# Gathers of blocks 1 and 2 in fives, block 1 transposed one step later, and smaller rings, in a recommender kernel

## The chip, the cores and the metric

One core of a Trainium2 chip runs the whole kernel in one launch. The time is device time in microseconds; a profiled execution gives the span of the core's instructions and a little around it. Engines: TensorE (PE) for matmuls, its weight loads apart (PEld), VectorE (DVE), ScalarE (ACT), GpSimd (POOL), and SyncE (SP), which here only issues DMAs. ACT and GpSimd issue DMAs too. Each engine runs its instructions in the order of the program, and they wait for one another through semaphores, which a finished instruction or a landed DMA increments.

## The reference

512 rows, each with 39 indices into a table of 125000 x 16. The gathered table rows `e` (512 x 39 x 16) feed three branches, which one output layer joins:

```python
e = emb_table[feat_index]                                  # (512, 39, 16)
flat = e.reshape(512, -1)
linear_part = flat @ linear_w + linear_b
x0 = e
h1 = relu(einsum('bhd,bmd,ohm->bod', x0, x0, conv_w1) + conv_b1)    # 128 maps
nxt, hi1 = split(h1, 2, axis=1)
h2 = relu(einsum('bhd,bmd,ohm->bod', nxt, x0, conv_w2) + conv_b2)
res = concatenate([hi1, h2], axis=1).sum(axis=2)
y = relu(bn(flat @ deep_w1 + deep_b1)); y = relu(bn(y @ deep_w2 + deep_b2))
out = concatenate([linear_part, res, y], axis=1) @ out_w + out_b
```

`bn` is a batch norm over all 512 rows. All is fp32. An index that is out of the table is wrapped and clamped.

## The kernel before, in words

The batch is cut into 8 blocks of 64 rows; a block is 1024 columns (16 dimensions x 64 rows), so a tile is 128 partitions x 1024 fp32, and a matmul goes over it in two halves of 512.

**How a block comes in.** GpSimd issues 20 indirect DMAs per block (`gather`, L509), each of 128 table rows, into one half of `G`, which has two rooms. PE transposes `G` in three pieces (`transposes`, L707), ACT copies them out to `xT` and `flatT` and writes `xT` to a scratch tensor in device memory (`out_of_transposes`, L899). From there `load_fields` reads it back with six DMAs (`load_x`, L442): twice into `x2`, four times into `xa`, the fields stacked on partitions. `x2` is cut in a high and a low part (`high_x` on ACT, `low_x` on DVE or GpSimd) in `stack`, so that a matmul with a 0/1 matrix `put1` or `put2` can copy chosen fields to any partitions of `p_x` without loss (`place`, L736).

**The products.** The first einsum of a block is six tiles of kind `x`: PE places the partners in PSUM, DVE multiplies them by `xa` into the ring `placed` (`product`, L620), and PE contracts the tile with the weights into `p_n` (`contract`, L758). The squares go in apart (`squares`). ACT then takes `p_n` out in three instructions (`hi_out_of_l1`, `second_n`, `first_n`), the last of which gives the second einsum its factor. The second einsum of a block is 20 tiles. Most are of kind `d`: SP loads two fields from the scratch tensor, each spread over 64 partitions, into the ring `ring` (L486 to L499), DVE multiplies the tile in place by `p_n`, PE contracts it into `p_h2`. A few are of kind `p`: PE places the fields, ACT copies them into `placed` (`copy_fields`).

**Split tiles.** A tile is contracted either as plain fp32 or split: ACT makes a rounded high part `zh` (`high_part`), DVE or GpSimd the rest `zl` (`low_part`), and PE does three fast matmuls per half in place of one fp32 one. `DVE_LOW` and `POOL_LOW` say which places of a step are split, and on which engine.

**The order.** It is written out by hand. Stage -1 is the six x tiles of block 0. Step j (0 to 7) is the 20 tiles of block j's second einsum, mixed with the six x tiles of block j+1 at the places `X_AT[j]`; `P_AT[j]` are the places of kind `p`. Every engine walks through the same sequence of 208 tiles and does its further work at a place: (j, n) means place n of step j. `T_AT`, `T1_PE`, `T1_ACT`, `XA1_ACT`, `HIGH_X1_ACT` and `LOW_X1` place the arrival of a block: in the kernel before, block 1 is transposed at place 4 of stage -1, by PE and ACT, and its loads stand at place 5 there, behind it on ACT's queue. `D1` to `D2E` place the deep layers. PE places tiles ahead of their use, by a plan made at build time from these tables (L864 to L874).

**GpSimd's start.** It waits for the indices, issues the 40 gathers of blocks 0 and 1 one after another, waits for the transposes of block 0, and issues the 20 of block 2 (L531 to L537). Blocks 3 to 7 are gathered inside the steps, block b spread over places 2 to 24 of step b-3, its first one behind the transposes of block b-2. A DVE or PE instruction behind a semaphore waits in the queue of its engine, so everything behind it waits too; SP stops its ring loads behind the seventh until block 1 stands in the scratch tensor (L495).

Of the kernel before, what the change touches and what calls it, by code (L numbers as in the profile page):

```python
# [21 lines left out]
HALF_F = (FIELDS + 1) // 2  # L22
# [45 lines left out]
def runs(values, after):  # L68

    out = []  # L70
    for p, v in enumerate(values):
        if p and after(values[p - 1]) == v:
            out[-1][1] += 1
        else:
# [20 lines left out]

X_AT = {0: [6, 7, 9, 12, 16, 17], 1: [1, 2, 9, 11, 13, 15], 2: [0, 2, 5, 8, 10, 13], 3: [0, 2, 5, 8, 10, 13],
        4: [0, 2, 5, 8, 10, 13], 5: [0, 4, 7, 9, 12, 14], 6: [0, 2, 4, 6, 8, 10], 7: []}
P_AT = {0: [20, 24], 1: [17, 20, 25], 2: [17, 19, 25], 3: [17, 19, 25], 4: [17, 19, 25], 5: [], 6: [], 7: []}  # L100

DVE_LOW = {-1: [], 0: [3, 8, 13, 24], 1: [3, 12, 25], 2: [12, 20, 25], 3: [12, 20, 25], 4: [12, 20, 25],
           5: [1, 15, 23, 25], 6: [1, 12, 22, 25], 7: [0, 3, 6, 10, 27]}
POOL_LOW = {-1: [], 0: [14, 23], 1: [0, 4, 8, 10, 16, 20], 2: [1, 3, 7, 16, 19, 24], 3: [1, 3, 7, 16, 19, 24],
# [3 lines left out]

SQ_AFTER = 3


T_AT = {0: 10, 1: 6, 2: 6, 3: 6, 4: 6, 5: 6}
T_AHEAD, XA_BEHIND, HIGH_X_BEHIND, LOW_X_BEHIND = 4, 7, 11, 12
LOW_X_ON_DVE = [3]

T1_PE, T1_ACT, XA1_ACT, HIGH_X1_ACT, LOW_X1 = (-1, 4), (-1, 4), (-1, 5), (0, 2), (0, 2)
SQ_ACT_AHEAD, SQ_DVE_AHEAD = 5, -1
HI_BEHIND, DUP_BEHIND, N_BEHIND, HI_SUM_BEHIND, H2_PLACE, H2_SUM_PLACE = 3, 7, 8, 5, 1, 6
LOW_BEHIND, COPY_AHEAD, PLACE_AHEAD = 1, 3, 6
RING, PLACED_RING, HIGH_RING, LOW_RING = 9, 4, 6, 5  # L120

FIRST_LOADS = 7
D1 = [(5, 13), (5, 17), (6, 13), (6, 17)]
D1B = [(5, 20), (5, 23), (6, 20), (6, 23)]
D1S = [(5, 22), (5, 25), (6, 22), (6, 23)]
D1E = [(6, 23), (6, 25), (6, 26), (6, 26)]
D2 = [(7, -1), (7, 3), (7, 4), (7, 6)]
D2B = [(7, 6), (7, 7), (7, 9), (7, 11)]
D2S = [(7, 7), (7, 9), (7, 10), (7, 12)]
D2E = [(7, 13), (7, 12), (7, 13), (7, 14)]  # L130

# [4 lines left out]
def order_of(j):  # L136

    if j < 0:
        return [('x', 0, t) for t in range(X_TILES)]
    xs, ps = X_AT[j], dict(zip(P_AT[j], range(L2_TILES - len(P_AT[j]), L2_TILES)))  # L140
    loaded = iter([t for t in [TAIL, *range(L2_PAIRS)] if t not in ps.values()])
# [21 lines left out]

DVE_SPLITS = [s for s, (j, n) in enumerate(WHERE) if n in DVE_LOW[j]]
POOL_SPLITS = [s for s, (j, n) in enumerate(WHERE) if n in POOL_LOW[j]]
SPLITS = sorted(DVE_SPLITS + POOL_SPLITS)
# [19 lines left out]
def build(nc, idx, emb, lin_w, lin_b, w1a, w1b, b1, w2, b2, dw1, db1, g1, be1, dw2, db2, g2, be2,  # L186
# [12 lines left out]
    with ctx:  # L199
# [85 lines left out]
        s_gather = [sem("s_gather0"), sem("s_gather1")]  # L285
# [6 lines left out]
        s_tp = sem("s_tp")  # L292
# [42 lines left out]
        def own_wait(eng, semaphore, value):  # L335

            eng.wait_ge(semaphore, value)
            eng.sem_inc(s_past, 1)
# [48 lines left out]

        T_PE = {b: (b - 2, T_AT[b - 2] - T_AHEAD) for b in range(2, BLOCKS)}
        T_ACT = {b: (b - 2, T_AT[b - 2]) for b in range(2, BLOCKS)}
# [118 lines left out]
        def _(pool):  # L508
            def gather(b, f):  # L509

                nc.gpsimd.indirect_dma_start(  # L511
                    G[:, b % 2, DIM * f:DIM * (f + 1)], None, emb[:, :],
                    bass.IndirectOffsetOnAxis(idx_all[:, b, f:f + 1], 0)).then_inc(s_gather[b % 2], 16)
# [15 lines left out]
            nc.gpsimd.affine_select(out=ident[:, :], in_=ident[:, :], compare_op=ALU.not_equal, fill=1.0,  # L529
                                    base=0, pattern=[[-1, 128]], channel_multiplier=1).then_inc(s_ident, 1)  # L530
            pool.wait_ge(s_clamp, 3)  # L531
            for b in range(2):
                for f in range(HALF_F):
                    gather(b, f)
            own_wait(pool, s_tp, 1)
            for f in range(HALF_F):
                gather(2, f)  # L537

            works = each(LOW_X_POOL, low_x)
            for s, (j, n) in enumerate(WHERE):  # L540
# [556 lines left out]
```

## Time and profile before

| what | us |
|---|---|
| three runs | 499.76, 503.05, 506.67 (median 503.05) |
| profiled execution, in all | 504.29 |
| its span | 502.5 |
| PE busy | 414.9 (83%) |
| DVE busy | 370.7 (74%) |
| GpSimd (POOL) busy | 337.6 (67%) |
| ACT busy | 195.1 (39%) |
| mean granted TensorE clock | 0.948 |
| read from device memory | 88.37 MB |

The page cuts the span in 40 slices of 12.6 us; a digit is a tenth of a slice that the engine was busy, or a tenth of full clock that PE was granted. "Idle before" stands in brackets behind an instruction, with what ended it; `issue` means that the engine waited for nothing that the profile shows, and `remote` that a semaphore came whose sender the profile can't name. In a row `x4` after PE counts matmul records; an fp32 tile has four, a split one six.

### The profile page before, as it was taken

How to read it: one execution, taken by the hardware profiler on the slowest of the kernel's cores; microseconds unless marked ns; L12 is line 12 of the kernel's file. 1: busy time of each engine (PE TensorE's matmuls, PEld its weight loads, DVE VectorE, ACT ScalarE, POOL GpSimd, SP SyncE). 2: the span in 40 equal slices, each digit the busy share in tenths (PEclk: the TensorE clock that was granted, in tenths of full speed). 3: DMA queues.
4: the chain of work that ended last, by engine and by line, in shares of the span. 5: the costliest groups of instructions: out<-in, count | busy, mean ns of one | idle time of the engine just before them, and what ended most of it. 6: DMA issues, size and time to landing. Idle time of an engine off the chain costs nothing.

```text
span 502.5 us, 4581 instructions
## 1 busy us (share of the span) xinstructions
PE 414.9 (83%) x1248; PEld 232.1 (46%) x1248; DVE 370.7 (74%) x354; ACT 195.1 (39%) x242; POOL 337.6 (67%) x236
## 2 busy tenths in 40 slices
PE   0004622499999999999999999999999999999985
PEld 0002210145545655555555555564556665655713
DVE  5303010389779799889989989998878899899931
ACT  1202000333255164245415450734336357576431
POOL 5777774055776885878688868861555189867690
PEclk9999955599999999999999999999999999999978
DMA  3936831498999988899989999998786989999400
GB/s 72 170 42 149 183 49 5 102 224 192 223 218 201 235 209 199 199 199 241 218 185 218 219 227 174 230 242 220 190 209 170 237 209 229 241 253 255 125 1 0
DMA packets 42398, 89.99 MB, mean 179 GB/s; under 512 B 16012, under 2 KB 21451, under 8 KB 42372
## 3 DMA queue, kind: packets, MB, share of 16 engines
q1 hardware_dynamic: 28637, 80.28, 64.5%
q0 software_dynamic: 5120, 1.32, 7.3%
q10 hardware_dynamic: 8615, 8.09, 7.1%
q8 instruction: 10, 0.16, 0.2%
q14 instruction: 16, 0.13, 0.1%
HBM read 88.37 MB, written 1.28 MB: 178 GB/s over the span
## 4 chain that ended last, share of the span: by engine, by line
PE 60%; issue 10%; another core or an unknown queue 9%; DVE 8%; ACT 5%; SPq 3%; DMA 3%; POOL 2%; ACTq 0%; DVEq 0%; POOLq 0%
PE p_h L775 34%; PE p_n L775 13%; PE p_x L754 4%; DVE ring L643 4%; PE p_x L839 3%; PE p_n L839 3%; POOL zl L525 2%; SPq L453 1%; DVE placed L643 1%; DMA x<-xs_scratch 1%; ACT zh L958 1%; PE p_n L854 1%; DMA w2s<-in_w 1%; DVE zl L612 1%
## 5 line engine op out<-in xcount | busy, mean ns | idle before, releaser
L511 POOL DMA_INDIRECT G<-in_emb,idx_all x160 | 167.8, 1049 | 55.9 <-issue 43.0
L525 POOL TENSOR_TENSOR zl<-ring,zh 128x1024 fp32r<-128x1024 f32 x60 | 145.5, 2440 | 82.5 <-ACT zh L958 78.2
L643 DVE TENSOR_TENSOR ring<-p_n,ring 128x1024 f32<-128x1024 f32 x146 | 172.5, 1215 | 10.4 <-ACT p_n L984 9.4
L958 ACT ACTIVATE zh<-ring 128x1024 fp32r<-128x1024 f32 x83 | 87.0, 1056 | 122.1 <-DVE ring L643 84.2
L775 PE MATMUL p_h<-ring,w2s 128*128 128x512 f32 x252 | 118.0, 602 | 6.9 <-DVE ring L643 6.9
L775 PE MATMUL p_n<-placed,w1s 125*128 125x512 f32 (+2 forms) x192 | 95.0, 620 | 9.6 <-DVE placed L643 9.6
L643 DVE TENSOR_TENSOR placed<-xa,p_x 125x1024 f32<-125x1024 f32 (+2 forms) x45 | 54.6, 1214 | 37.5 <-remote 15.1
L775 PEld LDWEIGHTS p_h<-ring,w2s 128*128 128x128 f32 x252 | 48.4, 193 | 57.8 <-issue 45.3
L775 PE MATMUL p_h<-zh,w2l 128*128 128x512 f32 x184 | 68.6, 454 | 2.0 <-ACT h2s L992 0.7
L754 PE MATMUL p_x<-stack,put 103*125 103x512 f32 (+3 forms) x118 | 52.5, 527 | 10.3 <-issue 10.3
L775 PE MATMUL p_h<-zh,w2h 128*128 128x512 f32 x184 | 57.9, 396 | 0.0
L775 PEld LDWEIGHTS p_n<-placed,w1s 125*128 125x128 f32 (+2 forms) x192 | 37.8, 198 | 42.7 <-issue 28.1
L775 PE MATMUL p_h<-zl,w2h 128*128 128x512 f32 x168 | 54.0, 403 | 4.0 <-POOL zl L525 2.7
L775 PEld LDWEIGHTS p_h<-zh,w2l 128*128 128x128 f32 x184 | 33.9, 189 | 22.5 <-issue 11.9
L612 DVE TENSOR_TENSOR zl<-ring,zh 128x1024 fp32r<-128x1024 f32 x20 | 38.8, 1938 | 2.7 <-ACT zh L958 2.7
L775 PEld LDWEIGHTS p_h<-zh,w2h 128*128 128x128 f32 x184 | 34.6, 188 | 8.4
L775 PEld LDWEIGHTS p_h<-zl,w2h 128*128 128x128 f32 x168 | 30.9, 188 | 14.0 <-POOL zl L525 5.7
L754 PEld LDWEIGHTS p_x<-stack,put 103*125 103x125 f32 (+3 forms) x118 | 22.0, 191 | 31.6 <-issue 26.9
L714 PE MATMUL p_x<-ident,G 128*128 128x128 f32 (+1 forms) x21 | 3.8, 295 | 34.1 <-DMA G<-in_emb,idx_all 34.1
L973 ACT ACTIVATE placed<-p_x 128x1024 f32<-128x1024 f32 x14 | 14.4, 1027 | 35.1 <-PE p_x L754 27.5
L647 DVE TENSOR_REDUCE h_sum<-h2s 128x64 f32<-128x1024 f32 x8 | 15.5, 1937 | 15.2 <-ACT h2s L992 15.2
L518 POOL TENSOR_TENSOR stack<-x,stack 39x1024 fp32r<-39x1024 f32 x6 | 14.3, 2380 | 13.1 <-ACT stack L949 12.1
(95 smaller groups left out, 299.7 us busy)
## 6 DMA issues: line engine op xcount, KB each, us to landing
ring<-xs_scratch SPq DMA_DIRECT2D x292, 256.0 KB
xa<-xs_scratch ACTq DMA_DIRECT2D x21, 156.0 KB
G<-in_emb,idx_all POOLq DMA_INDIRECT x160
x<-xs_scratch ACTq DMA_DIRECT2D x14, 156.0 KB
xs_scratch<-xT ACTq DMA_DIRECT2D x16, 64.0 KB
dw_sb<-in_dw SPq DMA_DIRECT2D x4, 200.0 KB
xa<-xs_scratch SPq DMA_DIRECT2D x3, 156.0 KB
xa<-in_dw ACTq DMA_DIRECT2D x2, 156.2 KB
```

Of the source, the lines that this page charges most:

```text
L453: eng.dma_start(dst[p:p + n, t, :], src[row:row + n, tile, :]).then_inc(s_w, 16)
L511: nc.gpsimd.indirect_dma_start(G[:, b % 2, DIM * f:DIM * (f + 1)], None, emb[:, :], bass.IndirectOffsetOnAxis(idx_all[:, b, f:f + 1], 0)). ...
L518: nc.gpsimd.tensor_tensor(stack[0:FIELDS, b % 3, :], x2[0:FIELDS, :], stack[0:FIELDS, b % 3, :].bitcast(F32), ALU.subtract).then_inc(s_low ...
L525: nc.gpsimd.tensor_tensor(low_of(s), z_of(s), high_of(s).bitcast(F32), ALU.subtract).then_inc(s_low_pool, 1)
L612: nc.vector.tensor_tensor(low_of(s), z_of(s), high_of(s).bitcast(F32), ALU.subtract).then_inc(s_low_dve, 1)
L643: nc.vector.tensor_tensor(z_of(s), by, x, ALU.mult).then_inc(s_z, 1)
L647: return nc.vector.tensor_reduce(dst[:, ROWS * b:ROWS * (b + 1)], src.rearrange("p (d b) -> p b d", d=DIM), AX.X, ALU.add)
L754: last = nc.tensor.matmul(acc[0:rows_of(s), BANK * c:BANK * (c + 1)], put, stack[:, b % 3, BANK * c:BANK * (c + 1)], start=True, stop=True)
L775: return nc.tensor.matmul(acc[:, BANK * c:BANK * (c + 1)], w, x[:, BANK * c:BANK * (c + 1)], start=start, stop=stop)
L839: last = nc.tensor.matmul(p_d[0:end - HID_K * t, :], w[:, HID_K * t:end], x, start=c == 0, stop=c == len(parts) - 1)
L958: nc.scalar.activation(high_of(s), z_of(s), ACT.Copy).then_inc(s_zh, 1)
L973: nc.scalar.activation(z_of(s), p_x[:, :], ACT.Copy).then_inc(s_copy, 1)
```

## The change

GpSimd's gathers of blocks 1 and 2 go in groups of five (`AT_ONCE`): before each group but a block's first it waits until all gathers of the block so far have landed. Block 0 is gathered as before. Block 1 is transposed at place 0 of step 0 by PE and ACT, no longer at place 4 of stage -1; its loads, high part and low part come at places 2, 4 and 4 of step 0. The x tiles of block 1, the transposes of block 2 and the places of later work move with it. Blocks 1, 3 and 7 have their low part of `x2` on DVE, not block 3 alone. Step 0 has no split tile on GpSimd any more, step 1 three in place of six; entries beyond a step's last place do nothing, so that 88 tiles are split in place of 92. `ring` has 8 rooms in place of 9, `placed` 2 in place of 4, and ACT copies a `p` tile 2 places ahead in place of 3.

```diff
-X_AT = {0: [6, 7, 9, 12, 16, 17], 1: [1, 2, 9, 11, 13, 15], 2: [0, 2, 5, 8, 10, 13], 3: [0, 2, 5, 8, 10, 13],
+X_AT = {0: [5, 10, 12, 14, 16, 17], 1: [5, 6, 9, 11, 13, 15], 2: [0, 2, 5, 8, 10, 13], 3: [0, 2, 5, 8, 10, 13],
         4: [0, 2, 5, 8, 10, 13], 5: [0, 4, 7, 9, 12, 14], 6: [0, 2, 4, 6, 8, 10], 7: []}
-P_AT = {0: [20, 24], 1: [17, 20, 25], 2: [17, 19, 25], 3: [17, 19, 25], 4: [17, 19, 25], 5: [], 6: [], 7: []}
-
-DVE_LOW = {-1: [], 0: [3, 8, 13, 24], 1: [3, 12, 25], 2: [12, 20, 25], 3: [12, 20, 25], 4: [12, 20, 25],
-           5: [1, 15, 23, 25], 6: [1, 12, 22, 25], 7: [0, 3, 6, 10, 27]}
-POOL_LOW = {-1: [], 0: [14, 23], 1: [0, 4, 8, 10, 16, 20], 2: [1, 3, 7, 16, 19, 24], 3: [1, 3, 7, 16, 19, 24],
-            4: [1, 3, 7, 16, 19, 24], 5: [3, 8, 11, 13, 16, 19, 21, 22, 24],
+P_AT = {0: [21, 24], 1: [16, 20, 25], 2: [17, 20, 25], 3: [17, 20, 25], 4: [17, 20, 25], 5: [], 6: [], 7: []}
+
+DVE_LOW = {-1: [], 0: [3, 6, 8, 13, 24], 1: [2, 12, 25], 2: [12, 20, 25], 3: [12, 20, 25], 4: [12, 20, 25],
+           5: [1, 15, 23, 25], 6: [1, 12, 22, 25], 7: [0, 3, 6, 10, 17]}
+POOL_LOW = {-1: [], 0: [], 1: [0, 10, 24], 2: [1, 4, 7, 14, 18, 24], 3: [1, 4, 7, 14, 18, 24],
+            4: [1, 4, 7, 14, 18, 24], 5: [3, 8, 11, 13, 16, 19, 21, 22, 24],
             6: [5, 7, 9, 11, 13, 14, 15, 16, 18, 19, 20, 21, 23, 24],
-            7: [1, 2, 4, 5, 7, 8, 9, 11, 12, 13, 15, 16, 17, 18, 19, 24]}
+            7: [1, 2, 4, 5, 7, 8, 9, 11, 12, 13, 14, 16, 18, 19, 24, 29]}
...
-T_AT = {0: 10, 1: 6, 2: 6, 3: 6, 4: 6, 5: 6}
+T_AT = {0: 15, 1: 3, 2: 6, 3: 6, 4: 6, 5: 6}
 T_AHEAD, XA_BEHIND, HIGH_X_BEHIND, LOW_X_BEHIND = 4, 7, 11, 12
-LOW_X_ON_DVE = [3]
-
-T1_PE, T1_ACT, XA1_ACT, HIGH_X1_ACT, LOW_X1 = (-1, 4), (-1, 4), (-1, 5), (0, 2), (0, 2)
+LOW_X_ON_DVE = [1, 3, 7]
+
+AT_ONCE = 5
+
+T1_PE, T1_ACT, XA1_ACT, HIGH_X1_ACT, LOW_X1 = (0, 0), (0, 0), (0, 2), (0, 4), (0, 4)
...
-LOW_BEHIND, COPY_AHEAD, PLACE_AHEAD = 1, 3, 6
-RING, PLACED_RING, HIGH_RING, LOW_RING = 9, 4, 6, 5
+LOW_BEHIND, COPY_AHEAD, PLACE_AHEAD = 1, 2, 6
+RING, PLACED_RING, HIGH_RING, LOW_RING = 8, 2, 6, 5
...
-D1E = [(6, 23), (6, 25), (6, 26), (6, 26)]
-D2 = [(7, -1), (7, 3), (7, 4), (7, 6)]
-D2B = [(7, 6), (7, 7), (7, 9), (7, 11)]
+D1E = [(6, 23), (6, 26), (6, 26), (6, 26)]
+D2 = [(7, -1), (7, 3), (7, 4), (7, 4)]
+D2B = [(7, 6), (7, 7), (7, 8), (7, 11)]
...
             pool.wait_ge(s_clamp, 3)
-            for b in range(2):
+            for b in range(3):
+                if b == 2:
+                    own_wait(pool, s_tp, 1)
                 for f in range(HALF_F):
+                    if b and f and f % AT_ONCE == 0:
+
+                        own_wait(pool, s_gather[b % 2], 16 * (HALF_F * (b // 2) + f))
                     gather(b, f)
-            own_wait(pool, s_tp, 1)
-            for f in range(HALF_F):
-                gather(2, f)
```

## Rows read from the trace of the kernel before

**Rows 1.** The page's slices: busy tenths of PE, and its granted clock.
```profile
PE   0004622499999999999999999999999999999985
PEclk9999955599999999999999999999999999999978
```
**Rows 2.** Stretches: length, each engine's busy time (instructions), granted clock, DMA share, GB/s.
```profile
108.40:149.14 40.74, 40.74 (x121) 22.16 (x120) 33.61 (x28) 14.33 (x20) 27.50 (x23) 1.00 0.95 213
...
97.00:103.00 6.00, 5.12 (x7) 2.25 (x8) 5.97 (x5) 0.08 (x1) 0.00 (x0) 0.56 0.94 210
```
**Rows 3.** The chain of waits in order of time: start, length, what.
```profile
46.89 43.39 another core or an unknown queue
```
**Rows 4.** Timeline of the hole: start, length, engine, line, operation, tiles, idle before.
```profile
53.20 1.03 PE L754 MATMUL p_x<-stack,put 103*125 103x512 f32 x2
55.38 1.03 PE L754 MATMUL p_h<-stack,put 103*117 103x512 f32 x2
69.85 1.22 DVE L643 TENSOR_TENSOR placed<-xa,p_x 125x1024 f32<-125x1024 f32 x1 [15.13 <-remote]
76.74 0.85 PE L714 MATMUL p_n<-ident,G 128*128 128x128 f32 x3
...
82.08 0.94 POOL L511 DMA_INDIRECT G<-in_emb,idx_all  x1 [0.30 <-issue]
85.95 1.22 DVE L643 TENSOR_TENSOR placed<-xa,p_h 117x1024 f32<-117x1024 f32 x1 [13.75 <-remote]
90.31 0.59 ACT L903 ACTIVATE xT<-p_n 128x128 f32<-128x128 f32 x3 [43.42 <-remote]
```
**Rows 5.** Timeline: last gather of block 0, first of block 1, and early work.
```profile
31.02 0.94 POOL L511 DMA_INDIRECT G<-in_emb,idx_all  x1 [0.30 <-issue]
32.27 0.95 POOL L511 DMA_INDIRECT G<-in_emb,idx_all  x1 [0.31 <-issue]
34.07 0.87 PE L714 MATMUL p_x<-ident,G 128*128 128x128 f32 x3 [34.07 <-DMA G<-in_emb,idx_all]
48.51 1.22 DVE L643 TENSOR_TENSOR placed<-xa,p_x 125x1024 f32<-125x1024 f32 x1 [0.18 <-issue]
```
**Rows 6.** DMA from 0 to 57.05, then to 136.10: packets, MB, share; issues.
```profile
q0 software_dynamic: 1167, 0.30, 19.4%
...
q0 software_dynamic: 2348, 0.61, 14.0%
...
G<-in_emb,idx_all POOLq DMA_INDIRECT x78
```
**Rows 7.** The chain, PE's pieces: a placement, an unsplit tile, a split tile.
```profile
110.58 0.46 PE p_x L754 x2
111.04 1.72 PE p_h L775 x4
...
116.99 1.41 PE p_h L775 x6
```
**Rows 8.** Timeline: block 1 from the transposes' copy to its stack and squares.
```profile
93.17 1.11 ACT L965 ACTIVATE hi<-p_n,b_sb 64x1024 f32<-64x1024 f32 x1 [1.61 <-issue]
94.56 17.19 SPq L498 DMA_DIRECT2D ring<-xs_scratch  x14
95.60 0.75 ACTq L445 DMA_DIRECT2D x<-xs_scratch  x2
96.60 4.62 DVE L643 TENSOR_TENSOR ring<-p_n,ring 128x1024 f32<-128x1024 f32 x4 [9.43 <-ACT p_n L984]
102.92 1.06 ACT L949 ACTIVATE stack<-x 103x1024 fp32r<-103x1024 f32 x1 [6.42 <-DMA x<-xs_scratch]
106.75 1.06 ACT L929 ACTIVATE hi<-xa 39x1024 f32<-39x1024 f32 x1 [1.83 <-DMA xa<-xs_scratch]
```
**Rows 9.** The page's groups: busy, mean ns of one, idle before.
```profile
L617 DVE TENSOR_TENSOR stack<-x,stack 39x1024 fp32r<-39x1024 f32 x2 | 3.5, 1750 | 17.3 <-issue 17.3
```
**Rows 10.** The waits, who waited for whom: us in total, times, longest.
```profile
DVE ring L643 <- DMA ring<-xs_scratch: 0.3, 1, 0.3
```

## The prediction

> **What bounds the kernel now.** I read the page's slices first, then stretches of the span, the chain of waits, and only then the timeline from 26 to 112 us. The slices show PE at 9 tenths from the ninth on, and nearly empty in the sixth and seventh, with the granted clock at 5 tenths there [rows 1]. From 108.40 to 149.14 us PE was busy 40.74 of 40.74 us [rows 2]: what lies behind the first 100 us is PE's, and there only less PE work takes time out. Ahead of it stands one hole: a single piece of the chain, 43.39 us from 46.89 us, with no releaser that the profile knows [rows 3].
>
> The timeline tells what kind of hole it is [rows 4]. PE placed x tile 4 from 53.20, 1.03 us long; DVE's product of it started at 69.85, 15.13 us idle before it. Tile 5 was placed from 55.38; its product started at 85.95. The transposes of block 1 ran at 76.74; ACT, which waited for them alone, started at 90.31. Each time the work was done 13 to 30 us before the waiter moved: signals from PE are held. What runs through all of it is GpSimd, which issues a gather each 1.25 us without a pause up to 82.08; all is free 8.2 us after that last one. Later, gathers run 7 to 10 in a row beside a PE without idle time, so gathers alone don't hold it; a long unbroken row may. That is inferred from order in time; no row shows the mechanism.
>
> **The change, part by part.** Sums are against the profiled execution: span 502.5 us, 504.29 us in all, 1.2 us over the median of 503.05.
>
> *Waits for each five.* Block 0 is gathered as before. Block 1 starts at 32.27. Five take 4 x 1.25 us to the fifth's issue, then its landing L. L from below: 3.05 us (issue 31.02, PE's start on it 34.07) [rows 5]. From above: by 136.10 us 78 gathers were issued and 2348 packets, of 32 each, seen, so 4.6 in flight, 5.8 us; by 57.05, under ring loads, 39 were issued (20 of block 0, then one each 1.25 us from 32.27) with 1167 packets, 2.5 in flight, 3.2 us and so some 3.5 with the last packets' way [rows 6]. I take 3.05 for block 1's first two fives, 3.5 for the others (nearest rows): fifths landed at 40.3, 48.5, 57.1, 65.7. Block 2 follows without a wait at its head: 72, 81, 90 and, with 5 us under full DMA, about 100, where it ended at 85 before. Those 15 us are GpSimd's; behind them in its queue stands only block 3, which it then issues in one run of 20, about 97 to 121, since step 0 has no low parts on GpSimd any more.
> Of waits behind a DMA the Trainium skill says, in DMA: Bandwidth & Descriptors, section Rules for kernel authors, to issue early and wait late, and gives some 2.0 us of fixed cost (section Anatomy of one DMA). By that alone six waits would be an estimated 12 us lost and nothing won; the rows agree that there is a fixed cost, at 3.05, not that it is on the path.
>
> *Stage -1 without the hole.* Placed x4 at 54.2, product 55 to 56.2, the squares' low part to 57.4, product 5 to 58.6. PE: tile 3 to 58.1, squares 0.5, tiles 4 and 5 at 1.72 us each [rows 7]: 62.0. A ring of two for placed tiles makes product s wait for PE's tile s-2, done one tile time before: nothing here, at most 1 us. ACT's three evictions of p_n take 3.4 us (93.17 to DVE's next start at 96.60) [rows 8]: 65.4, against 96.5 before. They no longer queue behind the wait for the transposes, which is moved past them. First product of step 0 to 66.6, PE to 68.4, transposes of block 1 to 69.1; its gathers landed at 65.7 (at 76 with L at 5.8 in all four).
>
> *Block 1 on its way.* ACT's four scratch writes landed 4.25 us after the transposes were seen (90.31 to SP's next load at 94.56). The six x loads, now behind tile 2 of step 0 on ACT's queue, gave x2 7.3 us after their issue (95.60 to 102.92), and xa 11.15 us (to 106.75) [rows 8]. SP's ring loads from the eighth on start at the same landing, as before. So 69.1 + 4.25 + 7.3 = 80.7; ACT's high part 1.06; low part, now DVE's, 1.75 [rows 9]: 83.5, xa at 84.5. PE gets to the first placement behind tile 2 of step 0, at about 72, and stands there until 84. This is the new stall, 12 us, and what is late in it are the x loads. It also halves the clock: after the old hole PE had 0.56 of it from 97 to 103, which costs 2.5 us, and I charge the same [rows 2].
>
> *Rest of step 0.* Old: behind 108.40 stood tiles 4 to 25, without a gap, to 149.14. New, from 84: tiles 3 to 25, one unsplit tile more (1.72), clock 2.5, transposes of block 3 0.3: 129.3. Gain 19.9. PE comes to the transposes of block 2 (place 11) at 84 + 3 x 1.41 + 6 x 1.72 + 4 x 0.46 + 2.5 = 103 [rows 7], gathers there at 100; to those of block 3 (place 25) at 129 against 121 + 5: both just hidden. If not, PE waits in order.
>
> *Edits with small terms.* Four split tiles less (one in step 0, inside the count above, three in step 1): an unsplit tile costs PE 1.72, a split one 1.41, so 0.9 us lost. Blocks 1 and 7's low part on DVE, and one split of step 7 moved to it, lie under PE. Ring 9 to 8: a load is issued one tile, about 2 us, later; DVE lost 0.3 us in all to ring loads [rows 10]; from 0 to 3 us lost, I take 1. Copying 2 ahead in place of 3, and the shifted places of steps 1 to 4: 0 to 1. The end (deep layer up to 2 places earlier, GpSimd one tile less): from 2 won to 1 lost, taken as 0.
>
> Sum: 19.9 - 0.9 - 1 = 18.0. Span 484.5, 486.3 in all, 485 on the median's scale. Its own bounds: x loads faster by 4 and the end by 2 give 478; the small losses at their ends and L somewhat longer give 490.
>
> **Rivals.**
> *1, slower: the signals stay held as long as block 2's gathers go on.* For it: two of PE's signals came through only behind the last gather, 3.9 and 8.2 us after its issue, while a pause after a five lasts just L. Against it: x tile 2 was signalled at once (product at 48.51, idle 0.18) in the middle of the same run [rows 5]. Price with the holding just as long as before: tile 5 of stage -1 ends at 91 and ACT's evictions come 2 us earlier; but the transposes stand behind the first tile of step 0, which at half clock ends near 99, so 10 later; the placement of block 1 comes at 114.5 and not 108.4, one tile more (1.7), clock 2.5, 0.9: 11 us lost, 515. With the waits the last issue of block 2 is 14 us later: 529. It decides at tile 5's product, about 59: if that comes after 90, it is this one.
> *2, no change: the run of 20 of block 3.* It has no wait, and PE is then in full stream. If holding starts inside it (from 103, say), PE loses up to 121 + 8.2 - 103 = 26 us, half of it in the middle: 498 (486 to 511). Against: runs of 7 to 10 with PE at 40.74 of 40.74 [rows 2]; for: nothing between 10 and the row of 60 was seen beside a busy PE. The Trainium skill, in VectorE: DVE Perf Modes, section The TRN2 errata, warns that increments at a high rate from one engine can deadlock another and wants them spaced; by that rule spacing blocks 1 and 2 is right and this unspaced run is the risk. The held signals agree in kind, though nothing hung.
> *3, the waits become the bound.* L near 5 in every five: block 1 late by 4 to 7, block 2 past PE at place 11 by 5: 496, between 490 and 500. For it: DMA is at 0.95 of its time from 108 on [rows 2].
>
> **Numbers.** My forecast 0.58, rival 3 0.11, rival 2 0.15, rival 1 0.16. Two per cent, 10 us, is about what a measurement here tells from no change: under 493 is faster, over 513 slower. Faster: 0.57 + 0.07 + 0.04 = 0.68; slower: 0.16 + 0.02 = 0.18; 0.14 between. The range from 477 to 508 takes the forecast, rival 3 and most of rival 2, and leaves rival 1 out.
>
> **What would show it.** In the new trace: gathers of blocks 1 and 2 in fives, with idle of about L released by the gather's DMA; products 4 and 5 before 60 us with no unknown releaser over 2 us; ACT's transposes of block 1 near 69; PE idle from about 72 to 84 for the stack of block 1, behind the loads of x; half clock for some 5 us behind it; eviction of step 0 near 130. The forecast is wrong if products 4 or 5 are still 10 us behind their placement, if PE shows idle released by nobody between 97 and 130, or if PE waits for G at places 11 or 25.

## The result, and the profile after

The changed kernel took 521.24 us (median of four runs, 518.87 to 523.54) against 504.83 for the kernel before beside it: a ratio of 1.033 with a 95% interval of 1.029 to 1.038. It is slower by 16.4 us, where 18 less were forecast, and the range of 477 to 508 missed it. The profiled execution took 521.02 us in all, with a span of 519.2. Lines of the changed kernel are 2 to 4 higher than before's: the gather is L513, the transposes L718, a placement L758, VectorE's product L647, ScalarE's copy of a placed tile L977.

The hole that the prediction was about is gone. Its slices against [rows 1]:

```profile
PE   0005754839389999999999999998999999979975
PEclk9999977987879999999999999999999999979988
```

PE is no longer near empty in the sixth and seventh slice (5 and 4 tenths for 2 and 2), but the ninth and eleventh stand at 3, where before's are at 9. The stretch that was full before [rows 2] shows it (length, busy time of PE, PEld, DVE, ACT, POOL, granted clock, DMA share, GB/s):

```profile
108.40:149.14 40.74, 21.44 (x48) 10.82 (x49) 13.19 (x12) 4.41 (x10) 23.85 (x25) 0.75 0.41 70
```

PE is busy 21.4 of 40.7 us at 0.75 of its clock. The chain of waits says behind what, in place of the one piece of [rows 3] (start, length, what):

```profile
46.74 8.24 DMA G<-in_emb,idx_all
...
61.62 3.04 DMA G<-in_emb,idx_all
...
70.45 3.00 DMA G<-in_emb,idx_all
...
81.38 11.15 DMA xa<-xs_scratch
...
120.46 22.96 another core or an unknown queue
```

The timeline gives the rest (start, length, engine, line, operation, tiles, idle time before it and who ended it). It answers [rows 4, 5, 8]:

```profile
55.65 1.22 DVE L647 TENSOR_TENSOR placed<-xa,p_x 125x1024 f32<-125x1024 f32 x1 [0.96 <-PE p_n L779]
55.78 0.94 POOL L513 DMA_INDIRECT G<-in_emb,idx_all  x1 [8.09 <-DMA G<-in_emb,idx_all]
57.92 1.21 DVE L647 TENSOR_TENSOR placed<-xa,p_h 117x1024 f32<-117x1024 f32 x1
...
73.58 0.53 PE L718 MATMUL p_n<-ident,G 128*128 128x128 f32 x3 [3.03 <-DMA G<-in_emb,idx_all]
74.14 0.59 ACT L907 ACTIVATE xT<-p_n 128x128 f32<-128x128 f32 x3 [8.44 <-PE p_n L718]
...
86.64 1.22 PE L758 MATMUL p_x<-stack,put 103*125 103x512 f32 x2 [7.40 <-issue]
92.62 1.22 DVE L647 TENSOR_TENSOR placed<-xa,p_x 125x1024 f32<-125x1024 f32 x1 [6.04 <-DMA xa<-xs_scratch]
95.53 0.94 POOL L513 DMA_INDIRECT G<-in_emb,idx_all  x1 [8.12 <-DMA G<-in_emb,idx_all]
107.74 0.94 POOL L513 DMA_INDIRECT G<-in_emb,idx_all  x1 [4.87 <-DMA G<-in_emb,idx_all]
116.78 0.87 PE L718 MATMUL p_x<-ident,G 128*128 128x128 f32 x3 [8.44 <-DMA G<-in_emb,idx_all]
...
128.51 0.73 PE L758 MATMUL p_x<-stack,put 103*128 103x512 f32 x2 [0.70 <-issue]
138.62 0.94 POOL L513 DMA_INDIRECT G<-in_emb,idx_all  x1 [0.30 <-issue]
143.55 1.02 ACT L977 ACTIVATE placed<-p_x 128x1024 f32<-128x1024 f32 x1 [24.60 <-remote]
144.62 1.22 PE L758 MATMUL p_x<-stack,put 103*128 103x512 f32 x2 [10.22 <-ACT placed L977]
```

Four things are to be seen. The products of x tiles 4 and 5 run at 55.65 and 57.92 and not at 69.85 and 85.95: the old hold is gone. The wait for a five to land is 3 us in some places and 8 us in others. PE waits for block 2's gathers until 116.78. And from 107.74 GpSimd issues 25 gathers in a row (the last five of block 2, the twenty of block 3), and there a tile that PE had placed by 129.24 is copied only at 143.55, 4.9 us behind the last issue: the hold of the kernel before, in a new place. The copy waits for two counts of PE, that of the placed tile and that of the product which last used its room; in the second trace of the changed kernel the tile, placed by 129.98, was counted at 140.03, and the copy started at 143.66 with the last of three late counts of products (143.54 to 143.66). With a `placed` ring of 2 that product is a newer one than with 4; what this adds was not tried apart. The waits together (who waited for whom; total us, times, longest):

```profile
POOL G L513 <- DMA G<-in_emb,idx_all: 29.9, 6, 8.1
ACT placed L977 <- remote: 24.6, 1, 24.6
PE p_n L843 <- DMA G<-in_dw: 3.1, 1, 3.1
```

The last tile of step 0 ends at 158.88 (before: 149.14), that of step 1 at 208.66 (197.06), that of step 6 at 454.57 (441.65), the last of all at 511.98 (495.23). So 9.7 us are lost by the end of step 0, 3.2 in steps 1 to 6, 3.8 in step 7.

Of the kernels below, three had executions over 1.5% above their fastest, at much the same granted clock (before with six waits on PE's signals: 508.4 and 511.75 us beside 494.0 to 496.21; before with more such waits: 503.72 beside 495.44 to 501.67; the changed kernel waiting for the five before the last: 526.72 beside 518.76 to 526.28); the medians below take them in, the ratios leave them out, and the traces of the first two are of such executions.

### The profile page after: what moved, and what is told of

It reads as the page before. It is cut to its first block, busy times and chain, and to the rows that moved or that the text cites. A ratio compares the mean times of both kernels' runs of the same rounds, so it can differ in the third digit from the quotient of the medians.

```text
span 519.2 us, 4551 instructions
## 1 busy us (share of the span) xinstructions
PE 423.6 (82%) x1240; PEld 233.6 (45%) x1240; DVE 376.6 (73%) x358; ACT 190.8 (37%) x238; POOL 320.0 (62%) x228
## 4 chain that ended last, share of the span: by engine, by line
PE 51%; issue 12%; DVE 11%; POOL 9%; DMA 9%; another core or an unknown queue 4%; ACT 3%; ACTq 1%; DVEq 0%; POOLq 0%
PE p_h L779 29%; PE p_n L779 9%; POOL G L513 7%; DVE ring L647 6%; PE p_x L758 4%; DMA G<-in_emb,idx_all 3%; PE p_x L843 3%; PE p_n L843 3%; DMA G<-in_dw 3%; DMA xa<-xs_scratch 2%; DVE placed L647 2%; POOL zl L527 2%; ACT zh L962 1%; DVE zh L611 1%
## 5 line engine op out<-in xcount | busy, mean ns | idle before, releaser
L513 POOL DMA_INDIRECT G<-in_emb,idx_all x160 | 168.5, 1053 | 76.4 <-issue 41.0
L527 POOL TENSOR_TENSOR zl<-ring,zh 128x1024 fp32r<-128x1024 f32 x58 | 141.3, 2450 | 110.0 <-ACT zh L962 103.4
L647 DVE TENSOR_TENSOR ring<-p_n,ring 128x1024 f32<-128x1024 f32 x146 | 172.9, 1215 | 11.1 <-ACT p_n L988 7.7
L962 ACT ACTIVATE zh<-ring 128x1024 fp32r<-128x1024 f32 x80 | 83.9, 1055 | 154.5 <-DVE ring L647 120.2
L779 PE MATMUL p_h<-ring,w2s 128*128 128x512 f32 x264 | 128.3, 620 | 4.8 <-DVE ring L647 4.8
L779 PE MATMUL p_n<-placed,w1s 125*128 125x512 f32 (+2 forms) x192 | 92.8, 608 | 0.0
L647 DVE TENSOR_TENSOR placed<-xa,p_x 125x1024 f32<-125x1024 f32 (+2 forms) x45 | 54.6, 1213 | 41.7 <-PE p_x L758 16.6
L779 PEld LDWEIGHTS p_h<-ring,w2s 128*128 128x128 f32 x264 | 52.3, 200 | 57.2 <-issue 48.2
L758 PE MATMUL p_x<-stack,put 103*125 103x512 f32 (+3 forms) x118 | 51.5, 519 | 30.1 <-ACT placed L977 10.4
L779 PE MATMUL p_h<-zh,w2h 128*128 128x512 f32 x176 | 55.9, 399 | 0.0
L779 PE MATMUL p_h<-zl,w2h 128*128 128x512 f32 x160 | 52.2, 408 | 2.9 <-POOL zl L527 2.8
L758 PEld LDWEIGHTS p_x<-stack,put 103*125 103x125 f32 (+3 forms) x118 | 22.0, 195 | 52.6 <-issue 34.3
L616 DVE TENSOR_TENSOR zl<-ring,zh 128x1024 fp32r<-128x1024 f32 x19 | 30.3, 1595 | 15.8 <-issue 9.6
L718 PE MATMUL p_x<-ident,G 128*128 128x128 f32 (+1 forms) x21 | 4.2, 317 | 42.5 <-DMA G<-in_emb,idx_all 42.5
L977 ACT ACTIVATE placed<-p_x 128x1024 f32<-128x1024 f32 x14 | 14.4, 1025 | 40.0 <-remote 24.6
L647 DVE TENSOR_TENSOR placed<-p_n,placed 128x1024 f32<-128x1024 f32 x14 | 17.0, 1217 | 16.1 <-ACT placed L977 13.3
L718 PEld LDWEIGHTS p_x<-ident,G 128*128 128x128 f32 (+1 forms) x21 | 2.7, 148 | 46.0 <-issue 45.7
```

The source lines that it names most:

```text
L513: nc.gpsimd.indirect_dma_start(G[:, b % 2, DIM * f:DIM * (f + 1)], None, emb[:, :], bass.IndirectOffsetOnAxis(idx_all[:, b, f:f + 1], 0)). ...
L527: nc.gpsimd.tensor_tensor(low_of(s), z_of(s), high_of(s).bitcast(F32), ALU.subtract).then_inc(s_low_pool, 1)
L616: nc.vector.tensor_tensor(low_of(s), z_of(s), high_of(s).bitcast(F32), ALU.subtract).then_inc(s_low_dve, 1)
L647: nc.vector.tensor_tensor(z_of(s), by, x, ALU.mult).then_inc(s_z, 1)
L718: last = nc.tensor.transpose(room_of_t(b)[0:r, 128 * q:128 * (q + 1)], G[:, b % 2, 128 * q:128 * q + r], ident[:, :])
L758: last = nc.tensor.matmul(acc[0:rows_of(s), BANK * c:BANK * (c + 1)], put, stack[:, b % 3, BANK * c:BANK * (c + 1)], start=True, stop=True)
```

## The experiments

Every kernel was compared with the kernel before on the same chip. That turned out to matter most: before itself took 504 to 506 us in four of the six comparisons and 485 to 486 in two. I call the first kind held and the second free; one chip was met in both kinds, so it is not the chip alone. Pairs of one program in both kinds say where the difference sits. The changed kernel without waits ends step 0 at 133.00 us in its free trace and at 162.49 in its held one, and from there to the end of step 6 it takes 295.3 and 295.9 us. So it is not a clock or a memory that is slower throughout. Medians in us, ratios with 95% intervals:

| kernel | free: this / before | held: this / before |
|---|---|---|
| changed kernel | not run | 521.24 / 504.83, 1.033 [1.029, 1.038]; 521.19 / 504.4, 1.032 [1.028, 1.036] |
| changed, no waits between fives | 493.8 / 485.37, 1.017 [1.010, 1.023] | 525.78 / 504.4, 1.043 [1.038, 1.048] |
| changed, wait for the five before the last | not run | 523.93 / 504.4, 1.030 [1.025, 1.036] |
| changed, block 3 behind VectorE's products | 508.16 / 485.37, 1.043 [1.036, 1.050] | 519.71 / 505.84, 1.026 [1.019, 1.033] |
| changed, block 3 in fives too | 516.99 / 485.37, 1.062 [1.055, 1.070] | 519.1 / 505.03, 1.028 [1.023, 1.033] |
| changed, no waits, rings and tail of before | not run | 520.49 / 505.84, 1.025 [1.016, 1.033] |
| changed, waits on PE's signals instead | not run | 503.49 / 505.03, 0.999 [0.996, 1.002] |
| before, with the waits between fives | 509.85 / 485.37, 1.047 [1.039, 1.055] | 511.66 / 505.84, 1.010 [1.007, 1.013] |
| before, six waits on PE's signals | 487.2 / 486.01, 1.003 [1.000, 1.006] | 496.21 / 505.84, 0.978 [0.969, 0.986] |
| before, more such waits | 490.12 / 486.01, 1.010 [1.006, 1.013] (tighter ones) | 498.77 / 505.03, 0.987 [0.980, 0.995] |

**Block 3 in fives too.** Theory A was then: a long row of gathers holds PE's signals, always.

```diff
                     if f == 0:
                         own_wait(pool, s_tp, b - 1)
+                    if b == 3 and f and f % AT_ONCE == 0:
+                        own_wait(pool, s_gather[b % 2], 16 * (HALF_F * (b // 2) + f))
                     gather(b, f)
```

> The changed kernel with block 3's gathers in fives too, each five waiting for the last to land. Theory A (PE's signals arrive late while GpSimd issues a long unbroken row of gathers, and a pause lets them through): no signal of PE is late by over 3 us between 120 and 145, the waits of 24.6 and 12.75 us on the placed tile go, and the time is 505 to 512 against 521. Rival B (the late signals come from the new order of the work or from the smaller rings): the hold stays and the time is 518 to 524. Rival C (the landing waits themselves are what costs): three more waits of 3 to 8 us each delay block 3 as well, and the time is 520 to 530.

516.99 us, 6.2% over a before of 485.37. No signal was held, as A says, but the time is not A's; and since nothing was held in this comparison even in long rows (next kernel), the absence says nothing for A.

**No waits at all.** `AT_ONCE = 100`: order, places and rings of the change alone.

> The changed kernel without its waits between fives: the new order and the rings of 8 and 2 alone, and 60 gathers of blocks 1, 2 and 3 in one row. Theory A: one hold from about 54 to the end of the row (31 + 60 x 1.25 = 106, plus 5 to 8), so 108 to 114, some 20 us longer than before's, and the time is 524 to 545. Rival B (order and rings cost, the waits do not matter): 518 to 524, with PE going on by 90. Rival C (the landing waits are the cost): faster than the changed kernel, 500 to 515.

493.8 us, rival C's side, and theory A falls with it. GpSimd issued 63 gathers in one row from 28.03 to 109.19, the longest of all, and nothing was held (timeline):

```profile
54.51 1.22 DVE L647 TENSOR_TENSOR placed<-xa,p_h 124x1024 f32<-124x1024 f32 x1 [1.74 <-PE p_n L779]
56.70 1.22 DVE L647 TENSOR_TENSOR placed<-xa,p_x 125x1024 f32<-125x1024 f32 x1 [0.96 <-PE p_n L779]
58.97 1.21 DVE L647 TENSOR_TENSOR placed<-xa,p_h 117x1024 f32<-117x1024 f32 x1
72.69 0.94 POOL L513 DMA_INDIRECT G<-in_emb,idx_all  x1 [0.30 <-PE p_n L718]
109.19 1.96 POOL L513 DMA_INDIRECT G<-in_emb,idx_all  x1 [0.30 <-issue]
```

**The kernel before with the waits of the change**, its order and rings kept.

```diff
-            for b in range(2):
+            for b in range(3):
+                if b == 2:
+                    own_wait(pool, s_tp, 1)
                 for f in range(HALF_F):
+                    if b and f and f % 5 == 0:
+                        own_wait(pool, s_gather[b % 2], 16 * (HALF_F * (b // 2) + f))
                     gather(b, f)
```

> The kernel before with the waits between fives in blocks 1 and 2 alone; order, places and rings stay as before. Theory A: the hold to 86 to 90 goes, but PE meets the transposes of block 1 ahead of the products and waits for their landing until about 72 to 75, 14 us earlier than before; some of it is given back at block 2's transposes: 490 to 502. Rival B (order and rings cost some 15 us and the waits none): 485 to 490. Rival C (the landing waits cost as much as the hold): 503 to 512.

509.85 against 485.37: the waits alone cost 24 us where nothing is held. That is in rival C's band of 503 to 512, but not by its argument, since there was no hold whose gain they could have eaten up.

**Block 3 behind VectorE's products.**

```diff
+                    if b == 3 and f % 2 == 0:
+                        own_wait(pool, s_z, s - 1)
                     gather(b, f)
```

> The changed kernel with block 3's gathers in twos, each two waiting for VectorE's product two places before theirs, and not for a landing. Theory A: the row of 25 is broken without any landing wait, no signal of PE is late by over 3 us after 120, and the time is 503 to 511. Rival B: hold stays, 518 to 524. Rival C (landing waits): 505 to 515 only if the fives of blocks 1 and 2 are what costs, otherwise unchanged.

508.16, inside theory A's 503 to 511, but by luck: the pacing bound nothing. In the trace the 25 gathers from 107.15 to 139.00 still stand in one row, no idle time over 0.31 us in it, and no signal was held all the same. So this kernel stands for the changed kernel in a free comparison, where that one was not run: it too would be 4.3% slower than before. Against the kernel without waits (493.8) in the same comparison, the landing waits of blocks 1 and 2 cost 14.4 us where nothing is held, and block 3's (516.99) another 8.8.

**The same kernels where before takes 504.** Because before had been 19 us faster than ever, the next four were forecast by a new theory, A2: whether signals are held in a long row is a property of the comparison, not of the code.

> The kernel before, unchanged, profiled beside the others on one chip, since before took 485 us beside the last four kernels and 504 beside the changed kernel. Theory A2 (the hold of PE's signals is not a property of the row of gathers alone: it appears on some chips and not on others): where before takes 483 to 489 its trace has no stretch in which ScalarE and VectorE wait for a remote signal, and stage -1 ends by 80 and not 91; where it takes 500 to 507 the hold is there. Rival (the chips differ in clock or DMA alone): the hold is in both, and the 19 us are spread over the span.

504.01, and the hold is there: `ACT xT L903 <- remote` 43.2 us, 43.4 in the first trace.

> The changed kernel, unchanged, beside before on the same chip. Theory A2: on a chip without the hold it has no 24.6 us wait for a remote signal, and takes 506 to 511, as the kernel with block 3's gathers paced by VectorE (508), which differs in that alone: ratio 1.04 to 1.05. On a chip with the hold: 519 to 523 against 500 to 507. Rival (the hold is the row's own): 521 on any chip.

521.19: the loss of the first comparison, repeated.

> The new order and rings without the waits between fives, once more, beside before and the changed kernel. Theory A2: without a hold 493 to 496, and the waits alone are then 13 to 15 us of the loss; with a hold (chip of the first comparison) 60 gathers in a row make it 520 to 540. Rival (landing waits cost nothing, order and rings do): within 1% of the changed kernel.

525.78, 32 us more than the same program in the free comparison. Its timeline, to be laid beside the one above:

```profile
62.08 1.22 DVE L647 TENSOR_TENSOR placed<-xa,p_h 124x1024 f32<-124x1024 f32 x1 [10.15 <-issue]
78.18 1.22 DVE L647 TENSOR_TENSOR placed<-xa,p_x 125x1024 f32<-125x1024 f32 x1 [14.88 <-remote]
87.98 1.22 DVE L647 TENSOR_TENSOR placed<-xa,p_h 117x1024 f32<-117x1024 f32 x1 [7.46 <-remote]
...
103.09 0.95 POOL L513 DMA_INDIRECT G<-in_emb,idx_all  x1 [20.49 <-PE p_n L718]
```

Three products stand 7.6, 21.5 and 29.0 us later than there, behind the same gathers 1.25 us apart. The waits between fives gain 4.6 us here (525.78 to 521.19); they take the first hold out and pay it back.

> The changed kernel, but each five waits for the five before the last one (never over 10 gathers on their way, no pause for a landing), in blocks 1, 2 and 3. Where an issue takes 1.25 us and a landing 3 to 9, the wait binds little: 494 to 500 on a chip without the hold if the landing waits are what costs; 506 to 511 if any limit on gathers on their way costs as much; on a chip with the hold 515 to 540.

The gathers of each five signal one of two semaphores in turn, and GpSimd waits for the five before the last. It waited for landings 3.3 us in all, and the time stayed at 523.93: a bound on gathers on their way that lets GpSimd go on issuing frees nothing. Its first 43 gathers (28.1 to 81.9) stayed one row.

**The fives of before, again, now beside a held before.**

> The kernel before with the landing waits in fives for blocks 1 and 2 alone, once more for the other kind of chip (510 against 485 on the first). Theory A2: where before takes 500 to 507, it takes the same 506 to 513, since it has no long row left and so no hold: the 43 us wait for a remote signal is gone and the landings cost what it gave. Rival (order or place, not the row, makes the hold): 520 or more, with waits for a remote signal in stage -1.

511.66, and 509.85 in the free comparison: with no long row left it hardly matters which kind it is, which is what A2 said. The rival is out. Some counts of PE are late in this held trace too, behind its rows of 8 and 10, but by little (a tile placed by 124.56 was counted at 125.86), and no wait for a remote signal on a tile or a copy stands in it. What it pays is in its timeline:

```profile
56.21 0.94 POOL L511 DMA_INDIRECT G<-in_emb,idx_all  x1 [8.47 <-DMA G<-in_emb,idx_all]
73.13 0.87 PE L715 MATMUL p_n<-ident,G 128*128 128x128 f32 x3 [11.91 <-DMA G<-in_emb,idx_all]
108.71 2.35 POOL L518 TENSOR_TENSOR stack<-x,stack 39x1024 fp32r<-39x1024 f32 x1
111.11 1.22 PE L755 MATMUL p_x<-stack,put 103*125 103x512 f32 x2 [20.17 <-POOL stack L518]
```

PE waits 11.9 us at the transposes for block 1's landing, and 20.2 us for block 1's low part of x, which stands on GpSimd's queue behind all the waits. The change had moved that part to VectorE.

**Block 3 behind VectorE, again.**

> The changed kernel with block 3's gathers in twos behind VectorE's products, once more for the other kind of chip (508 on the first). Theory A2: where the changed kernel takes 519 to 523, the row of 25 is what holds the signals from 128 to 143, and pacing it gives 505 to 511. Rival (the pacing does not pause GpSimd long enough): 517 to 523 with the wait of 20 us or more for a remote signal still there.

519.71: a miss for A2. The waits were met when GpSimd reached them, so the row was never broken (106.52 to 138.44, no idle time over 0.31 us in it), and the hold stayed:

```profile
143.42 1.02 ACT L979 ACTIVATE placed<-p_x 128x1024 f32<-128x1024 f32 x1 [24.71 <-remote]
```

The same program with the same row, free and then held, is the clearest sight of what a hold takes (stretches as above):

```profile
124.00:144.40 20.40, 20.39 (x53) 9.66 (x52) 17.47 (x15) 8.37 (x8) 14.03 (x14) 1.00 0.74 151
124.00:144.40 20.40, 9.44 (x25) 4.13 (x23) 5.06 (x5) 0.98 (x1) 11.72 (x13) 0.86 0.26 31
```

Step 0 ends at 144.39 in the free trace and at 158.69 in the held one; step 1 gives 2.3 us of that back.

**Rings of 9 and 4 and the tail's loads of before, no waits.**

```diff
-RING, PLACED_RING, HIGH_RING, LOW_RING = 8, 2, 6, 5
+RING, PLACED_RING, HIGH_RING, LOW_RING = 9, 4, 6, 5
...
-D1E = [(6, 23), (6, 26), (6, 26), (6, 26)]
-D2 = [(7, -1), (7, 3), (7, 4), (7, 4)]
-D2B = [(7, 6), (7, 7), (7, 8), (7, 11)]
+D1E = [(6, 23), (6, 25), (6, 26), (6, 26)]
+D2 = [(7, -1), (7, 3), (7, 4), (7, 6)]
+D2B = [(7, 6), (7, 7), (7, 9), (7, 11)]
```

> The changed kernel without its waits, and with the rings of 9 and 4 and the four loads of the tail placed as in before: what is left of the change is the order of the tiles and splits. If rings and tail cost most of the 8.4 us between this order without waits (494) and before (485) on a chip without the hold: 485 to 488 there, and 517 to 522 against 526 on a chip with it. If the order costs it: 492 to 495, or 524 to 528.

520.49, in the band of "rings and tail", and 5.3 us under the kernel without waits (525.78, in another held comparison). Where they lie isn't shown. By the step ends 2.1 us are in step 0, where two different holds stand, and 3.0 in step 7 (55.6 us long against 58.6). But step 7 of one program varies as much between traces: 53.6, 54.7 and 56.3 us in the three of before, 55.5 and 58.6 in the two of the kernel without waits.

**Waits on PE's own signals.** If a row must be broken only when signals are late, then GpSimd should wait for those signals: the wait is nothing where they are prompt.

```diff
+            PE_AT = {(1, 12): (s_place, 1), (1, 16): (s_mm, 1), (2, 4): (s_mm, 4),
+                     (2, 8): (s_tp, 2), (2, 12): (s_mm, 5), (2, 16): (s_mm, 6)}
+            for b in range(3):
+                if b == 2:
+                    own_wait(pool, s_tp, 1)
+                for f in range(HALF_F):
+                    if (b, f) in PE_AT:
+                        own_wait(pool, *PE_AT[b, f])
+                    gather(b, f)
```

> The kernel before with six waits on PE's own signals inside the gathers of blocks 1 and 2 (for a placed tile, a finished product, the transposes), each for a signal that is due by then, and none for a landing. Theory A2 (on some chips PE's signals are held while GpSimd issues without a pause, and any pause lets them through): where before takes 500 to 507, GpSimd stops after at most 12 gathers, the hold breaks up early, and the time is 484 to 494, the time of a chip without the hold; where before takes 483 to 489 the waits are met when they are reached: 483 to 490. Rival (only a quiet GpSimd and DMA frees the signals, as while a landing is waited for): each wait lasts 5 to 8 us and the time is 495 to 510 on a chip with the hold.

Three executions took 494.0 to 496.2 beside 505.84, 2.2% less than before and a little short of the expected 484 to 494; the two others took 508.4 and 511.75, more than before. So a gain is likely, but its size is open. The trace is of the execution of 508.4 us and shows the hold moved (to 90 to 112 us) and not gone: VectorE still waits for a remote signal for 20.3 us in three pieces, longest 11.8, where it was 28.9 in two, longest 15.1.

> The kernel before with waits on PE's signals after every fourth gather of blocks 1 (from its twelfth), 2 and 3, so no row is over 13 gathers until the last; each waits for a signal that is due some microseconds earlier. Theory A2: signals are prompt to the end of step 0, no wait for a remote signal is over 3 us, and beside a before of 500 to 507 the time is 482 to 491 (the six waits gave 494 to 496, with a row of 35 left in which signals were held); beside a before of 483 to 489 it is 483 to 491. Rival (only a landing wait frees the signals): 494 or more.

498.77: not the 482 to 491 of A2. In its trace (503.72 us) GpSimd still issued 25 gathers in a row (63.37 to 94.49), since the signals asked for had come before it got there, and VectorE has 14.4 us of remote waits. More waits than six won nothing that can be told.

> The changed kernel with the same kind of waits on PE's signals in place of its waits for landings: new order, rings of 8 and 2, no landing wait, no long row. Theory: the time is that of the order without waits where nothing was held, 491 to 497, whichever before stands beside it; order and rings cost 6 to 10 us against the kernel before with the same waits. Rival (order and rings cost nothing once no signal is held): within 3 us of that kernel.

503.49, where 491 to 497 were expected. Signals were held here too, in the row up to 56.26: GpSimd itself waited 5.4 us for a remote signal and VectorE 8.7. It is 17.7 us below the changed kernel with its landing waits (521.19, another held comparison), and 4.7 us above the kernel before with such waits (7.6 above that one's median without its slowest execution).

> The changed kernel with block 3's gathers in fives with landing waits, once more. Theory A2: 513 to 518 whichever before stands beside it, with no wait for a remote signal; beside a before of 500 to 507 that is 3 to 8 us less than the changed kernel. Rival (the hold after 120 has another cause): 520 to 530 beside a before of 500 to 507, with the remote wait there.

519.1, a little over the band of 513 to 518. The row of 25 is broken, and the wait of 24.6 us for a remote signal behind it is gone: without the row it does not come. The one of 4.6 us that is left ends at 198.57, 3.0 us behind the last of 13 gathers in a row (177.69 to 195.56), and so contradicts A2's "no wait". The time hardly follows, since each block now waits for landings, and it is nearly that of the free comparison (516.99), as for the fives of before (waits of this kernel):

```profile
PE p_x L720 <- DMA G<-in_emb,idx_all: 54.2, 3, 33.3
POOL G L513 <- DMA G<-in_emb,idx_all: 45.2, 9, 8.5
ACT placed L979 <- remote: 4.6, 1, 4.6
```

> The kernel before, for its trace beside these three. Where it takes 500 to 507, PE's placed tiles from the third on and its first products arrive in steps up to 30 us late until 90; where it takes 483 to 489, every signal of PE arrives within 0.1 us though GpSimd's row of 40 gathers is the same.

506.57, with the hold (`ACT xT L903 <- remote` 34.2 us).

> The kernel before with six waits on PE's signals in the gathers of blocks 1 and 2, once more in five rounds. Beside a before of 500 to 507: 494 to 498, ratio 0.975 to 0.985, the hold of stage -1 ended by 70 and a shorter one after it. Beside a before of 483 to 489: 484 to 489, ratio 1.00. Rival (the gain was chance): ratio above 0.99 beside a before of 500 to 507.

487.2 beside 486.01, ratio 1.003: where nothing is held, the six waits cost about 1 us.

```profile
POOL G L511 <- PE p_h L778: 0.9, 3, 0.3
POOL G L511 <- PE p_n L778: 0.6, 3, 0.3
POOL G L511 <- PE p_h L757: 0.3, 1, 0.3
```

Each of GpSimd's waits for PE ended in 0.3 us, its normal gap. This is also the nearest trace to a free kernel before, of which none was taken: step 0 ends at 130.65 and step 7 at 478.06, where the change without waits has 133.00 and 483.74. So order, rings and tail of the change cost some 5.7 us between these traces, 2.4 of them in step 0 and 2.9 in steps 1 to 6; by the medians of the free comparison it is 8.4 (493.8 against 485.37).

> The kernel before with ten or more waits on PE's signals in the gathers of blocks 1, 2 and 3, each for a signal that is due only just before it. Beside a before of 500 to 507: 485 to 494 if the signals still held after 70 cost what the wait for a remote signal shows (up to 14 us), 494 to 500 if the pauses themselves now cost as much, because signals that GpSimd waits for come late too. Beside a before of 483 to 489: 484 to 492.

490.12 beside 486.01: asking for the newest signal costs 4 us where nothing is held. Where something is held it has not run.

## Why the prediction was wrong, step by step

*What bounds the kernel* was read rightly for the case at hand: a hold of PE's signals, seen behind a long unbroken row. The prediction called it "inferred from order in time", and what is shown now is narrower: in a held comparison every late count of PE stands in a row of 7 or more gathers or within 9 us behind it, and the waits of over 10 us in rows of 25 and more; landing waits take them away (the fives of before: 511.66 and 509.85 in either kind); in a free comparison 63 gathers in a row hold nothing. The row is needed, and something else besides, which no trace names.

*Stage -1 without the hole* held to a microsecond or two: products at 55.65 and 57.92 (forecast 55 and 57.4), ScalarE's eviction at 62.38 (62.0). Rival 1 is false.

*Waits for each five* is the first step that failed, by the size of L, the landing. I took 3.05 and 3.5 us for block 1 and 5 for block 2, with 5.8 as the upper bound. Measured on the chain: 8.24 us for block 1's second five, 3.04 and 3.00 for the two behind it; the waits before 95.53 and 107.74 were 8.12 and 4.87. The upper bound was a mean over all gathers on their way; the fives that meet ring or x loads have the long landing, and a mean hides them: the DMA share was 1.03 from 46.70 to 55.00, where L was 8.24, and 0.17 from 61.60 to 64.70, where it was 3.04. Block 1 landed at 73.5 and not 65.7. The Trainium skill's advice in DMA: Bandwidth & Descriptors, section Rules for kernel authors, to issue early and wait late, is what these runs bear out: 14.4 us for the waits in the changed order, 24 in before's. The prediction had quoted it and set it aside, since no row showed the landing on the path.

*Block 1 on its way*: transposes at 73.58 for 69.1, the stack at 86.64 for 84, and xa, forecast at 84.5, at 92.6, because the last of its loads is issued at 81.38 and takes 11.15 us from there.

*Rest of step 0*, forecast to end at 129.3, ended at 158.88: 29.6 us more. PE came to block 2's transposes at 108.34 instead of 103 (5.3); it waited there for G (8.4), which is rival 3 and more; and from 116.78 the rest took 42.1 in place of 26.3 (15.8), which is the hold in block 3's row and the lower clock behind it, rival 2. That these 15.8 us are the hold is borne out by the free trace with the same row (the kernel paced behind VectorE), where the rest takes 27.2 us, from 117.23 to 144.39. I had given these two rivals 0.11 and 0.15 as if only one could come; they came together, with xa on top, since both start from the same change: later gathers push block 3's into one row beside PE's stream.

*"Runs of 7 to 10 beside a full PE"* was the row on which I weighed rival 2 down. A row of 25 is not like it. And the row did not show what I took from it: in the same trace PE's counts are late in those short rows too (a count of a placed tile, at 138.95, came at least 1.2 us late, and one of a product, at 121.66, at least 1.0). A busy PE shows only that nobody needed them. That step 0 had no low parts left on GpSimd was in the prediction, as a reason that the row is fast; it was the reason that it is unbroken.

*Small terms*: forecast 1.9 us with 0 for the end; measured 3.2 in steps 1 to 6 (2.9 between the two free traces) and 3.8 in step 7. Step 7 of one program differs by up to 3.1 us between traces, and by 0.4 between the two free ones, so the 3.8 are not shown to be the change's.

The hoped-for 18 us were not lost in one place: of 29.6 us in step 0, 13.7 went to landings (of gathers and of xa) and 15.8 to the same hold elsewhere. Nor was it bad luck in the kind of comparison. In a free one before itself takes 485, with little of a hole left to win back, and the kernel that stands for the changed one took 508.16 against 485.37. The medians split what that kernel lost beside a held before: order, rings and tail 8.4 us, landing waits 14.4, block 3's hold 11.6 (519.71 against 508.16), less the 20.5 us by which before itself is slower where signals are held (505.84 against 485.37), make 13.9 us (519.71 against 505.84). The changed kernel itself lost 16.4 and 16.8.

What stays open: what makes a comparison held or free. It is not the program and not the chip alone. One thing in the traces goes with the kind, though, and ties it to the gathers. In the six free traces nearly every increment that PE, VectorE or ScalarE makes has its count on record within 0.05 us. In the fourteen held ones many have none there: in the first trace of before 183 of the 324 that fall within 1.3 us behind the issue of a gather, 21 of 222 elsewhere, and none of the 311 behind the last gather at 332 us; in the free trace of before with six waits it is 3 of 342. So the kind can be read from any trace, also where nobody waits. A missing count need not have been late: PE had no idle time from 108.40 to 149.14 in that trace. Why counts are missing is open too.

## What to carry to other kernels

A wait for a landing costs the landing under the load of that moment, not the quiet one: read L from the stretch where other queues are busy, and from its longest, before putting such a wait into an issuing engine's queue. A stall that goes with an engine's long row of issues can come back wherever the next long row is, so count the rows of the changed schedule, not only the one removed; and a row is better broken by a wait on the signals that were late, which cost 1 us where they were not (4 us when it asked for the newest), than by a wait for a landing, which cost 14 to 24. Run the kernel before beside each candidate: here it moved by 19 us between comparisons, more than the change did.

## What the runs showed of the hardware

One program, the changed kernel without waits, had PE's semaphore increments counted within 0.02 us in one comparison (a product that ended at 51.33 counted at 51.35) and its products started up to 29 us later in another, while GpSimd issued indirect DMAs 1.25 us apart in both. In the first trace of before a tile placed by 54.22 was counted at 69.83 and one placed by 56.41 at 85.93, and in the row that the changed kernel starts at 107.03 in its second trace a product that ended at 108.43 was counted at 108.45, but a tile placed by 129.98 at 140.03. In all fourteen held traces the late counts are PE's alone; those of VectorE and ScalarE that are on record came promptly. An indirect gather of 128 rows took 2.6 to 3.1 us from issue to its last packet beside quiet queues, and up to 8.5 us beside ring or x loads (first trace of the changed kernel).
